# First attention stage: probabilities and values in fp16 halves, probabilities turned by DMA, quantised inputs in another order, routing last in TensorE's slot

## The reference, cut to what matters

```python
ln_out = _ln(hidden_states, ln_w, ln_b)
q  = _ln(_fp8_linear_pertensor(ln_out, wq, ...), qln_w, qln_b)     # 16 heads of 128
k  = _ln(_fp8_linear_pertensor(ln_out, wk, ...), kln_w, kln_b)     # 8 heads
v  =     _fp8_linear_pertensor(ln_out, wv, ...)                    # 8 heads
core = softmax(q k^T / sqrt(128)) v
qx = _ln(_fp8_linear_pertensor(ln_out, wqx, ...), ...)
kx, vx = split(cond @ w_kv_x.T); kx = _ln(kx)
xout = softmax(qx kx^T / sqrt(128)) vx
cat = concatenate([core, xout]);  catq = _div_clamp_fp8(cat, proj_smooth)
return catq @ wproj.T * (proj_in_scale * proj_w_scale)
```

## Time and profile before

| | us |
|---|---|
| median of 3 runs (range) | 3309.67 (3306.96 to 3312.15) |
| the profiled execution's own time | 3308.09 |
| its span, first to last instruction | 3305.9 |

### The profile page before, as it was taken

The page is one execution under the profiler, slowest core; times in us unless marked ns, Lnnn a source line. Parts: engine busy times, 40 slices in busy tenths (PEclk is TensorE's granted clock), DMA queues, the critical chain, the costliest instruction groups (busy, mean ns, idle before and its releaser), DMA issues. The chain is left out here.

```text
span 3305.9 us, 57383 instructions
## 1 busy us (share of the span) xinstructions
PE 2887.7 (87%) x16324; PEld 1656.1 (50%) x16325; DVE 1797.5 (54%) x5172; ACT 1695.5 (51%) x4502; POOL 1740.7 (53%) x2429
## 2 busy tenths in 40 slices
PE   4699999999999969999999997699899999634996
PEld 2366666666666635555555543344444444322663
DVE  3366656656666555343433444588888887321331
ACT  5577777777777623223332333466666666311332
POOL 6467766776677435345544543655555655241222
PEclk9899999999999989999999998899999999757998
DMA  6601100010011055445544565355545555327444
GB/s 239 223 27 36 49 29 29 35 51 29 29 35 45 30 192 155 134 134 160 153 135 133 159 183 134 74 107 106 108 105 109 109 104 106 101 84 273 85 83 105
DMA packets 459854, 348.33 MB, mean 105 GB/s; under 512 B 295728, under 2 KB 366512, under 8 KB 459696
## 3 DMA queue, kind: packets, MB, share of 16 engines
q1 hardware_dynamic: 396896, 267.79, 29.0%
q0 software_dynamic: 16640, 38.05, 5.7%
q10 hardware_dynamic: 46224, 41.36, 4.2%
HBM read 194.88 MB, written 93.50 MB: 87 GB/s over the span
## 5 line engine op out<-in xcount | busy, mean ns | idle before, releaser
L437 PE MATMUL a_mm<-a_w_hi,a_xq_hi 128*128 128x512 f16 x768 | 301.9, 393 | 65.2 <-POOL a_xq_lo L885 61.5
L1646 POOL TENSOR_TENSOR e_st<-e_st,e_ws_tile 128x1024 f32<-128x1024 f32 x64 | 123.7, 1933 | 429.8 <-PE e_y L1402 418.9
L601 DVE BATCH_NORM_STATS2 a_st<-a_mm 128x6 f32<-128x128 f32 x768 | 170.7, 284 | 326.1 <-PE a_mm L438 231.6
L750 ACT ACTIVATE a_nrm<-a_mm,a_sc_t 128x128 f32<-128x128 f32 x768 | 290.4, 472 | 106.3 <-POOL a_sc_t L903 106.1
L438 PE MATMUL a_mm<-a_w_hi,a_xq_lo 128*128 128x512 f16 x768 | 303.2, 395 | 0.0
L1440 ACT ACTIVATE e_hh<-e_ha 128x512 f16<-128x512 f32 x128 | 76.3, 596 | 415.8 <-PE e_ha L1387 414.4
L1535 DVE SCALAR_TENSOR_TENSOR e_hl<-e_ha,e_hh 128x512 f16<-128x512 f32 x128 | 88.4, 691 | 352.3 <-ACT e_hh L1440 351.8
L902 POOL TENSOR_TENSOR a_sc_t<-a_sc_t,a_mhalf 128x4 f32<-128x4 f32 x192 | 202.5, 1055 | 138.3 <-DVE a_sc_t L608 138.0
L1811 PE MATMUL a_mm<-l_wh,a_src_hi 128*128 128x512 f16 x512 | 200.1, 391 | 76.0 <-DVE a_vl L1893 41.7
L1400 PE MATMUL e_y<-e_w2h,e_hh 128*128 128x512 f16 x640 | 242.6, 379 | 0.0
L1401 PE MATMUL e_y<-e_w2l,e_hh 128*128 128x512 f16 x640 | 242.6, 379 | 0.0
(11 more groups left out here) (350 smaller groups left out, 8294.6 us busy)
## 6 DMA issues: line engine op xcount, KB each, us to landing
e_st<-in_w SPq DMA_DIRECT2D x128, 512.0 KB, 4.3
disp<-a_empty SPq DMA_DIRECT2D x16, 781.5 KB, 4.1
e_st<-in_w1b SPq DMA_DIRECT2D x32, 352.0 KB, 3.1
e_xb<-disp ACTq DMA_DIRECT2D x41, 260.5 KB
disp<-a_empty SPq DMA_DIRECT2D x4, 2605.0 KB, 21.5
e_xb<-disp SPq DMA_DIRECT2D x40, 260.5 KB, 4.4
a_cx<-in_ctxT SPq DMA_DIRECT2D x32, 256.0 KB, 3.2
a_stage<-in_wprojT SPq DMA_DIRECT2D x16, 512.0 KB, 4.8
```

The lines of the kernel that those rows point to most:

```text
L437: pe.matmul(out, xq_hi[:, n, c, :], w_hi[:, t, c, :], start=(c == 0), stop=False)
L750: ins = act.activation(nrm[:, n % 2, i * P:(i + 1) * P], src[:, i * P:(i + 1) * P], ACT.Identity, bias=sc_t[:, n % 2, 3, i:i + 1], scale=s ...
```

## The change

The probabilities are no longer transposed by TensorE. ScalarE makes the high fp16 half of the normalised probabilities times 1024 (`p_high`, offset 3, in the place of `p_keep`), VectorE the low half (`p_low`, offset 4, first in its plan), and SyncE turns both by DMA transposes (`p_turn`, offset 4). The values are kept as fp16 halves too: `v_keep` writes the high one, the new `v_low` on VectorE (one slot after the job) the low one, and only that frees the bank. `pv` does three fp16 matmuls for each of its two column halves and moves from offset 5 to 6; `o_quant` moves to 7, `out_project` to 10, and every "end" stage by one slot. All of TensorE's attention work is now in even slots. The sets are in the order K, Q, V, QX, so that set 1 (GpSimd's share) is Q and set 2 (ScalarE's) is V. The routing stages stand last in TensorE's plan; their waits and those of `x_transpose` are rewritten, since the bank PTB is now theirs alone.

```diff
-SETS = ["K", "V", "Q", "QX"]
+SETS = ["K", "Q", "V", "QX"]
+SCALE_OF = [0, 2, 1, 3]
...
+            def p_turn(b, a):
+                for half, done in ((0, "p_hi"), (1, "p_lo")):
+                    sp.wait_ge(sem[done], at(a, NA, b))
+                    if half == 0 and not (isinstance(b, int) and b == 0 and a < 2):
+                        sp.sem_inc(sem["turning"], 1)
+                        sp.wait_ge(sem["pv"], at(a - 2, NA, b))
+                    sp.sem_inc(sem["turning"], 1)
+                    sp.dma_start_transpose(pT[half][:, a % 2, :].rearrange("p (i t) -> p i t", t=P),
+                                           pq[half][:, a % 2, :]).then_inc(turned[half][a % 2], 16)
...
+            run_pipeline(sp, [("job", 0, lambda b, t: weights(b, t + 1)), ("att", 4, p_turn), ("att", 5, residual),
+                              ("end", 11, store), ("in", 1, x_load)],
...
-            def p_transpose(b, a):
-                pe.wait_ge(sem["pnorm"], at(a, NA, b))
...
-                for i in range(4):
-                    mm = pe.transpose(PTB[:, i * P:(i + 1) * P], pr[:, a % 2, i * P:(i + 1) * P], ident[:])
-                mm.then_inc(sem["ptr"], 1)
             def pv(b, a):
...
-                pe.wait_ge(sem["p_ok"], at(a, NA, b))
+                for half in range(2):
+                    pe.wait_ge(turned[half][a % 2], 16 * at(a // 2, NA // 2, b))
...
-                    mm = pe.matmul(OVB[:, i * 256:(i + 1) * 256], vt[:, KV_OF[a], g * P:(g + 1) * P],
-                                   pT[:, a % 2, i * 256:(i + 1) * 256], start=True, stop=True)
+                    pe.matmul(OVB[:, two], vh, ph, start=True, stop=False)
+                    pe.matmul(OVB[:, two], vh, pl, start=False, stop=False)
+                    mm = pe.matmul(OVB[:, two], vl, ph, start=False, stop=True)
...
-            run_pipeline(pe, [("end", 14, r_transpose), ("end", 16, r_logits), ("end", 20, r_prefix),
-                              ("job", 3, q_transpose), ("job", 0, project), ("att", 0, scores),
-                              ("att", 3, p_transpose), ("att", 5, pv), ("att", 9, out_project), ("in", 6, x_transpose)],
+            run_pipeline(pe, [("job", 3, q_transpose), ("job", 0, project), ("att", 0, scores),
+                              ("att", 6, pv), ("att", 10, out_project), ("in", 6, x_transpose),
+                              ("end", 15, r_transpose), ("end", 17, r_logits), ("end", 21, r_prefix)],
...
+            def v_low(b, t):
+                if t in v_no:
...
+                    dve.wait_ge(sem["v_hi"], at(v_no[t], NV, b))
+                    dve.scalar_tensor_tensor(out=vt[1][:, i, :], in0=MMB[BANK[t]][:], scalar=scal[:, col:col + 1],
+                                             in1=vt[0][:, i, :], op0=ALU.mult, op1=ALU.subtract).then_inc(sem["v_ok"], 1)
+
+            def p_low(b, a):
+                dve.wait_ge(sem["p_hi"], at(a, NA, b))
+                if not (isinstance(b, int) and b == 0 and a < 2):
+                    dve.wait_ge(turned[1][a % 2], 16 * at(a // 2 - 1, NA // 2, b))
+                dve.scalar_tensor_tensor(out=pq[1][:, a % 2, :], in0=pr[:, a % 2, :], scalar=PS, in1=pq[0][:, a % 2, :],
+                                         op0=ALU.mult, op1=ALU.subtract).then_inc(sem["p_lo"], 1)
...
+            run_pipeline(dve, [("att", 4, p_low), ("att", 2, row_scale), ("att", 1, smax), ("att", 7, o_quant),
+                               ("end", 11, final), ("end", 11, r_stats),
+                               *(("in", at_, x_quant_of(n)) for n, at_ in enumerate(X_QUANT_AT)), ("job", 0, stats), ("job", 1, v_low),
...
-            def p_keep(b, a):
-                act.wait_ge(sem["ptr"], at(a, NA, b))
+            def p_high(b, a):
+                act.wait_ge(sem["pnorm"], at(a, NA, b))
                 if not (isinstance(b, int) and b == 0 and a < 2):
-                    act.wait_ge(sem["pv"], at(a - 2, NA, b))
-                act.activation(pT[:, a % 2, :], PTB[:], ACT.Copy).then_inc(sem["p_ok"], 1)
+                    act.wait_ge(turned[0][a % 2], 16 * at(a // 2 - 1, NA // 2, b))
+                act.activation(pq[0][:, a % 2, :], pr[:, a % 2, :], ACT.Copy, scale=PS).then_inc(sem["p_hi"], 1)
```

More of the change, by code:

```diff
@@ L249, in layer0_attention @@
         kT = s.sb("kT", [P, 4, DM], F32)
-        vt = s.sb("vt", [P, 4, DM], F32)
+        vt = [s.sb(f"v{n}", [P, 4, DM], F16) for n in ("h", "l")]
         nb = s.sb("nb", [P, 2, 4], F32)
@@ L254, in layer0_attention @@
         pr = s.sb("pr", [P, 2, DM], F32)
-        pT = s.sb("pT", [P, 2, DM], F32)
+        pq = [s.sb(f"pq{n}", [P, 2, DM], F16) for n in ("h", "l")]
+        pT = [s.sb(f"p{n}", [P, 2, DM], F16) for n in ("h", "l")]
         oy = s.sb("oy", [P, 2, DM], BF16)
@@ L401, in x_transpose @@
                 pe.wait_ge(sem["x_norm"], b + 1)
[L402 to L405, removed]
+                if isinstance(b, int) and b == 0:
                     pe.wait_ge(sem["small"], 16 * N_SMALL)
+                if not (isinstance(b, int) and b < 3):
+                    pe.wait_ge(sem["r_lg"], b - 2)
                 for c in range(KT):
@@ L504, in out_project @@
                 mm.then_inc(sem["proj"], 1)
-            def kept(a, b):
-                return min(at(a, NA, b), NA * B) if isinstance(b, int) else at(a, NA, b)
             def r_transpose(b, k):
-                pe.wait_ge(sem["p_ok"], kept(4, b + 1))
-                if isinstance(b, int) and b == B - 1:
+                if not (isinstance(b, int) and b == 0):
                     pe.wait_ge(sem["r_pos"], b)
@@ L690, in x_quant_of @@
                 return lambda b, k: x_quant(b, n)
-            run_pipeline(dve, [("att", 2, row_scale), ("att", 1, smax), ("att", 6, o_quant), ("end", 10, final), ("end", 10, r_stats),
-                               *(("in", at_, x_quant_of(n)) for n, at_ in enumerate(X_QUANT_AT)), ("job", 0, stats),
-                               ("job", 0, convert), ("in", 3, x_stats), ("end", 16, r_scores), ("end", 18, r_pick),
-                               ("end", 20, r_slots)], NJ, SCORE_AT, ch, head=HEAD)
+            run_pipeline(dve, [("att", 4, p_low), ("att", 2, row_scale), ("att", 1, smax), ("att", 7, o_quant),
+                               ("end", 11, final), ("end", 11, r_stats),
+                               *(("in", at_, x_quant_of(n)) for n, at_ in enumerate(X_QUANT_AT)), ("job", 0, stats), ("job", 1, v_low),
+                               ("job", 0, convert), ("in", 3, x_stats), ("end", 17, r_scores), ("end", 19, r_pick),
+                               ("end", 21, r_slots)], NJ, SCORE_AT, ch, head=HEAD)
         @block.scalar
@@ L817, in _ @@
                                ("in", 9, convert_at(-1)), ("job", 3, q_keep), ("att", 1, exps), ("job", 1, normalise), ("job", 0, convert),
-                               ("att", 3, p_keep), ("job", 1, v_keep), ("in", 4, x_norm), ("in", 6, x_back),
-                               ("in", 8, y_part), ("in", NJ, ctx_split), ("end", 12, r_norm), ("end", 14, r_keep),
-                               ("end", 17, r_exp)], NJ, SCORE_AT, head=HEAD)
+                               ("att", 3, p_high), ("job", 1, v_keep), ("in", 4, x_norm), ("in", 6, x_back),
+                               ("in", 8, y_part), ("in", NJ, ctx_split), ("end", 13, r_norm), ("end", 15, r_keep),
+                               ("end", 18, r_exp)], NJ, SCORE_AT, head=HEAD)
         @block.gpsimd
```

44 lines of the change are left out of this document (18 added, 26 removed).

## The result

The changed kernel takes 3338.84 us (median of 4 runs, 3335.58 to 3343.18) beside 3310.13 for the kernel before in the same session: ratio 1.0091, interval 1.0078 to 1.0103. It is 0.9% slower, where 3% faster was forecast. The profiled execution's span is 3340.1 us, 34.2 more.

A forecast was written before the change was run, and what follows sets the result against it. TensorE was taken as the bound: pitch 66.58 to 58.1 + 0.8 + 0.7 = 59.6 us, 7.0 less over 14.65 batches; 3308.1 - 103 + 3 (start) + 4 (end) = 3212, as a median 3214 us. Range 3180 to 3275.

The forecast's parts named there:

- The floor of 58.1 us: Pitch of a batch on TensorE after gains of 3.4, 1.8 and 3.3 us from 66.6, before any new waits.
- The order of the inputs: Q's input made earlier: TensorE's 2.6 us wait and 0.7 us of slow clock go, 3.3 us per batch.
- routing last: nothing: Routing stages last in TensorE's slot and rewritten waits: no cost, bounds 0.3 either way.
- New waits, 0.8 + 0.7 us per batch: Added to the floor: 0.8 for the V bank, 0.7 for even and odd slots; upper bounds 6 and 2.6.
- the V bank: Values' bank, freed by v_low one VectorE instruction later, makes TensorE wait 0.8 us per batch; bounds 0 and 6.
- even and odd slots: TensorE's attention work all in even slots: job 15's bank and V0's input cost 0.7 us per batch; bounds 0 and 2.6.
- ScalarE: nothing: p_high replaces p_keep on ScalarE, 643 ns against 619: no cost; ScalarE at 86% of the floor pitch.
- The port: VectorE and GpSimd shut each other out of SBUF: each p_low could cost up to one GpSimd instruction (1.04 us) more.
- The turns: Sixteen DMA transposes per batch on SyncE's queue, 1.19 us each, landing after 2.5: no cost; bounds 0 and 2.5.
- Start: Turns between SyncE's weight loads and in front of a late input lengthen the start by 3 us; bounds 0 and 12.
- The slower one: Rival, chance 0.08: ring through p_low, statistics, scales and normalisation at worst times, 10.5 us; pitch 71.2, total 3382 us.
- A moved wait: Rival, chance 0.12: V's input or job 15's bank is late instead of Q's; pitch 62.9, total about 3261 us.

The follow-up runs named there:

- e9: Changed kernel, attention and end stages in their old slots, p_high right behind q_keep, p_low last, table fill in 20 pieces, x_stats first, ctx_low last: 3203.3 us, ratio 0.967.
- e13: Kernel before with the new order of inputs and the routing stages last in TensorE's slot: 3266.1 us, ratio 0.9859.
- e1: Kernel before with only the new order of inputs (K, Q, V, QX): 3324.9 us, ratio 1.0053.
- e2: Changed kernel with p_low last in VectorE's slot instead of first: 3337.0 us, ratio 1.0086.
- e3: Changed kernel with pv, o_quant, out_project and the end of a batch one slot later, putting pv and out_project in odd slots: 3357.7 us, ratio 1.0144.
- e14: Changed kernel with x_stats first in VectorE's slot and ctx_low last in GpSimd's, nothing else: 3301.3 us, ratio 0.9972.
- e17: Changed kernel, its slots kept, with table fill in 20 pieces, p_high right behind q_keep, p_low last, x_stats first, ctx_low last: 3254.5 us, ratio 0.9835.
- e18: e9 with p_high again behind the exponentials and the normalisation, as in the changed kernel: 3315.5 us, ratio 1.0018.
- e4: Changed kernel with the table fill cut into 20 pieces, one per slot: 3313.9 us, ratio 1.0017.
- e10: Kernel before with the table fill cut into 20 pieces, one per slot: 3292.8 us, ratio 0.9943.

## Why the prediction was wrong

*What bounds the kernel.* Right for the kernel before: TensorE. The floor of 58.1 us was right too as TensorE's own work: 57.9 in e9. That this floor would still be the bound was the error.

*What leaves TensorE.* Right. Six products in 0.66 us (timeline of TensorE in the changed kernel), and no transposes:

```profile
609.21 0.27 PE L487 MATMUL a_ovb<-a_ph,a_vh 128*128 128x256 f16 x1
...
609.87 1.03 PE L501 MATMUL a_prb<-a_wp,a_cq 128*128 128x512 f16 x4
```

*The order of the inputs.* The gain of 3.3 us is there (3.1, e13), but the step "routing last: nothing" was wrong: alone, the new order made the kernel slower (e1), since TensorE then stood 3.4 us per batch in front of the next blocking stage. The slow clock went with the wait only in e13 (1.00 in 400 to 1000 us); in the changed kernel it is 0.97, lower than before. The prediction named what was late, and didn't ask what is late next.

*New waits, 0.8 + 0.7 us per batch.* This step failed. It was 68.15 - 58.1 = 10.0 us, more than its two upper bounds together (6 + 2.6). TensorE's records show 7.5 of them as waits; most of the rest is TensorE busy for 60.3 us at a lower clock, which costs nothing by itself here (e2). I had priced the V bank at `v_low` and `p_low` at what stands behind it in its own ring. The bank hardly cost anything: TensorE waited once for `v_low` in the whole stage, 1.2 us at the start. Job 15's bank, in the step "even and odd slots", cost 2.07 us per batch by the trace, but e3 took most of it away and gained nothing. What I had not priced is work that feeds a third engine and stands late in a slot: `x_stats`, and through it 3.4 us of `x_scale` in front of the scales. It stood there before the change too, and cost nothing while TensorE was the bound. The two moved stages account for 2.4 of the 10.0 us (e14). The slots together with p_high's place account for 5.3 more (65.74 to 60.42, e14 and e9); there "even and odd slots", 0.7, and "ScalarE: nothing" were wrong together, and neither alone brings it (p_high early alone 0.9 us, e17; the old slots alone lose 2.5, e18). p_high costs what p_keep cost, 0.64 us, but its result now has two engines and a DMA to pass before TensorE, and it stood behind 3 us of other work. 2.3 us remain in the best version. Pitch 60.4 there is near the forecast of 59.6: the sum was that of a kernel whose stages stand in another order. That its total, 3203, is near 3214 is in part luck, since the fill in pieces, which the prediction didn't have, is in it.

*The port.* `p_low` came out at 671/691/1409 ns, under the 0.8 taken, and none of its 94 in 300 to 1100 us took over 0.70. The slow `q_low` of the earlier trace rows ran beside a GpSimd instruction of 1.26 us (L2103); that the excess is as long as the one of 1.04 in the earlier trace rows was chance. The contention showed on another instruction, the small `tensor_scalar` of the statistics (ns min/median/max; before, its maximum was 878 and its mean 297, now 513):

```profile
L600 DVE TENSOR_SCALAR a_sc_t<-a_mv,a_eps_s x141: 229/229/2377, 301.1 to 1093.1; 128x4 f32<-128x4 f32 x141
```

The longest began while a GpSimd DMA was being issued, ran beside two more GpSimd instructions and ended with the last:

```profile
606.61 2.37 DVE L600 TENSOR_SCALAR a_sc_t<-a_mv,a_eps_s 128x4 f32<-128x4 f32 x1
```

```profile
605.91 0.96 POOL L933 DMA_INDIRECT disp<-a_stage,a_sidx  x1 [0.30 <-issue]
606.90 1.05 POOL L879 TENSOR_TENSOR a_xqs<-a_y,a_isc 128x512 f32<-128x512 f16 x1
607.90 1.04 POOL L888 TENSOR_TENSOR a_xq_hi<-a_y,a_isc 128x512 f16<-128x512 f16 x1
```

The Trainium skill (SBUF — State Buffer, section Who interferes with whom) counts `tensor_scalar` among the operations that can take the shared pair of ports, and says that whoever issues first then has the pair for the whole instruction while the other is blocked. This trace agrees, by 2.37 us for a piece of 0.23. I had looked at the rule for the new instruction only. How much of the pitch it costs is not shown by any run.

*The turns.* 2.4 us to land, as taken, and no wait in the steady part. But the bound behind a fill was wrong at the start: the table fill of batch 0 was counted for the input and not for the turns, 17.0 us to land for one of them. *Start*: forecast 3, bound 12; measured 8.7 at the first projection of batch 2, all of it the turns behind the fill (e4 and e10). *End*: forecast 4 longer; from the last projection to the end of the last batch it is 28.5 us against 26.2, 2.3 longer. Both sizes were within their bounds; the loss is in the pitch.

*The rivals.* The slower one had the right picture (the engines besides TensorE set the pitch, through statistics, scales and normalisation) and the wrong link: p_low's place was not it (e2), and its price of 4.6 us per batch was three times the 1.6 measured. A moved wait did happen, in e1, but in routing, which the rival didn't name, and the change's own routing edit removed it. Of its two owners V's input is late by 7.1 us in nine waits, 0.6 per batch, and the bank of job 15 by 2.07 per batch; the second is near the size it named, but with most of it gone the pitch was no shorter (e3).

## What to carry to other kernels

Price a new instruction on an engine that works in order by everything that stands behind it in the slot, and look there for work that was ready and feeds a third engine, also where it stood late before and cost nothing. Here two stages that had only to stand elsewhere in their slot were worth 2.4 us per batch in the changed kernel and 4.3 in the old slots. When TensorE is relieved by 8% and the other engines are each at 60 to 75%, follow the chain again before taking the gain: here the bound moved to the hand-overs with no engine full. And where latency is added to a path, as by a turn by DMA, try its producer early in the slot before giving it more slots: here the first, in the old slots, was 5.3 us per batch better (e9 and e14).

## What the runs showed of the hardware that I had not expected

A DMA transpose issued behind 10.4 MB of plain writes on the same queue held the issuing engine for 10.26 us and landed after up to 17.0, against 1.19 and 2.4 us in the steady part. It isn't a matter of transposes: in the kernel before, a plain load in that place took 8.48 us to issue. With the writes cut in 20 pieces over 20 slots, the longest issue of a transpose was 2.48 us, the slowest landed after 7.5, and the pitch stayed at 68.3.
